# Decoder layer on one core: attention probabilities scaled by their row's reciprocal sum on GpSimd before the transposes, instead of the attention output scaled by transposed reciprocals

## What is computed

```
qp = q @ Wq.T                         # q: layernorm(x), 16 heads of 32
kv = latent_kv @ Wkv_expand.T         # the context; k, v = split(kv)
scores = einsum('bhqd,bhkd->bhqk', qh, kh) / sqrt(32), causal mask (512 x 512)
attn = softmax(scores, axis=-1)
out = einsum('bhqk,bhkd->bhqd', attn, vh)
return out @ Wout.T
```

## Time and profile before

| | |
|---|---|
| time, 3 runs | median 1807.98 us (1806.97 to 1808.12) |
| the profiled execution's own time | 1807.13 us |
| its span, first to last instruction | 1805.3 us |
| PE busy | 1412.3 us (78% of the span) |
| DVE busy | 1217.4 us (67%) |
| ACT busy | 842.5 us (47%) |
| POOL busy | 546.0 us (30%) |
| chain that ended last, by engine | PE 47%, DVE 25%, issue 9%, POOL 6%, ACT 5% |
| costliest lines of that chain | L513 9%, L1094 7%, L1111 7%, L1148 6%, L1171 6%, L1132 5%; L1120 has 2% |
| cross-attention stage of one batch, 605 to 701 us | PE busy 87.6 us, ACT 55.1, DVE 51.2, POOL 0.0 |

### The profile page before, as it was taken

The page is one execution under the profiler, slowest core; times in us unless marked ns, Lnnn a source line. Parts: engine busy times, 40 slices in busy tenths (PEclk is TensorE's granted clock), DMA queues, the critical chain, the costliest instruction groups (busy, mean ns, idle before and its releaser), DMA issues.

```text
span 1805.3 us, 31768 instructions
## 1 busy us (share of the span) xinstructions
PE 1412.3 (78%) x11547; PEld 875.8 (49%) x11616; DVE 1217.4 (67%) x2539; ACT 842.5 (47%) x2066; POOL 546.0 (30%) x494
## 2 busy tenths in 40 slices
PE   1224899779987899779887998779877988789866
PEld 0113665346644665446544664446544664456523
DVE  8993455975579555975578555965588556965565
ACT  2541354455634464445634554445544554445422
POOL 5881000650046101640046101640056002630054
PEclk9999799898989799898989799888989799889987
DMA  5311000010000000010000000010000000000000
GB/s 181 115 42 36 1 1 24 7 25 1 2 24 13 18 1 25 7 25 1 1 24 13 19 1 24 7 24 1 2 24 18 13 1 24 7 19 1 1 6 18
DMA packets 25287, 36.10 MB, mean 20 GB/s; under 512 B 2480, under 2 KB 10672, under 8 KB 25136
## 3 DMA queue, kind: packets, MB, share of 16 engines
q1 hardware_dynamic: 25136, 34.09, 7.0%
HBM read 25.69 MB, written 8.39 MB: 19 GB/s over the span
## 4 chain that ended last, share of the span: by engine, by line
PE 47%; DVE 25%; issue 9%; POOL 6%; ACT 5%; DMA 0%; SPq 0%; DVEq 0%; ACTq 0%; POOLq 0%
PE psum L513 9%; PE psum L1094 7%; PE psum L1111 7%; PE psum L1148 6%; PE psum L1171 6%; PE psum L1132 5%; DVE top L805 4%; DVE nmx L755 3%; DVE inter L831 3%; DVE xn L507 3%; PE psum L1097 2%; POOL iq L677 2%; DVE pt L768 2%; PE psum L1120 2%; DVE q L801 2%
## 5 line engine op out<-in xcount | busy, mean ns | idle before, releaser
L502 POOL TENSOR_TENSOR rstd<-var_eps,minus_half 128x1 f32<-128x1 f32 x96 | 55.2, 575 | 889.7 <-DVE var_eps L496 889.7
L953 ACT ACTIVATE p<-psum,nmx 128x384 f32<-128x384 f32 (+3 forms) x512 | 265.8, 526 | 68.8 <-DVE nmx L755 64.4
L755 DVE TENSOR_REDUCE nmx<-psum 128x2 f32<-128x256 f32 (+3 forms) x256 | 210.7, 823 | 115.7 <-PE psum L1097 115.6
L768 DVE COPY pt<-psum 128x128 f32<-128x128 f32 (+3 forms) x256 | 124.6, 487 | 194.0 <-PE psum L1111 193.5
L1111 PE MATMUL psum<-ident,p 128*128 128x128 f32 x1280 | 206.9, 289 | 19.6 <-ACT pt L977 16.4
L1094 PE MATMUL psum<-k_hl,q_hl 32*128 32x128 f32 (+3 forms) x1536 | 207.0, 377 | 15.4 <-DVE q_hl L742 11.7
L677 POOL TENSOR_TENSOR inter<-inter,rscale 128x512 f32<-128x512 f32 x128 | 140.0, 1094 | 205.0 <-DVE rscale L839 201.3
L977 ACT COPY pt<-psum 128x128 f32<-128x128 f32 (+3 forms) x256 | 109.2, 427 | 141.8 <-PE psum L1111 140.4
L1111 PEld LDWEIGHTS psum<-ident,p 128*128 128x128 f32 x1280 | 144.2, 146 | 54.6 <-ACT pt L977 25.8
L1171 PE MATMUL psum<-wg_sb,xq_t 128*128 128x512 bf16 x452 | 135.3, 421 | 37.8 <-ACT xq_t L984 24.7
L1094 PEld LDWEIGHTS psum<-k_hl,q_hl 32*128 32x128 f32 x1536 | 126.8, 203 | 76.6 <-issue 53.8
(11 more groups left out here) (102 smaller groups left out, 2497.5 us busy)
## 6 DMA issues: line engine op xcount, KB each, us to landing
x_in<-in_x_dram SPq DMA_DIRECT2D x32, 256.0 KB, 4.0
out_dram<-x_res SPq DMA_DIRECT2D x64, 128.0 KB, 2.4
w_raw<-in_w_gate_dram SPq DMA_DIRECT2D x16, 256.0 KB, 2.7
w_raw<-in_w_up_dram SPq DMA_DIRECT2D x16, 256.0 KB, 3.0
w_raw<-in_w_down_dram SPq DMA_DIRECT2D x16, 256.0 KB, 3.8
ctx_in<-in_ctx_t_dram SPq DMA_DIRECT2D x8, 256.0 KB, 3.0
wq_raw<-in_wq_t_dram SPq DMA_DIRECT2D x1, 1024.0 KB, 8.1
wo_sb<-in_wo_t_dram SPq DMA_DIRECT2D x1, 1024.0 KB, 10.1
```

Source lines behind the costliest of these rows:

```text
L755: dve.tensor_reduce(nmx2[:, u % UNITS, 2 * pr:2 * pr + 2], where(("scores2", oc, qt, pr))[:, :, 0:(qt + 1) * P], AX_X, ALU.max, negate=Tru ...
L768: free(dve.tensor_copy(pt2[:, hh, 0:m], where(label)[:, 0, 0:m]), label)
L953: ins = act.activation(p2[:, (4 * u + hh) % P2_RING, 0:m], where(label)[:, hh % 2, 0:m], ACT.Exp, bias=nmx2[:, u % UNITS, hh:hh + 1], accu ...
```

## The change

The probabilities are divided by their row sums before they are transposed, on GpSimd, in place in `p2`. DVE's `recips` takes a pair of heads at a time and signals GpSimd; GpSimd's new `scale_probs` multiplies each head's 128 x m tile by its column of reciprocals, and PE's transpose of a head waits for that head's product. The transposed reciprocals and all that served them are gone (`recip_x`, `recip_t`, `turn_recip`, `take_recip`, their places in slot C1); `take_out` becomes a copy. The ring `p2` has 8 places. On DVE the reciprocals of pair 1 of unit u now stand between `maxima(u+1, 0)` and `take_probs(u, 0)`, those of pair 0 of unit u+1 ahead of `maxima(u+1, 1)`.

```diff
@@ -38,7 +38,7 @@
...
 INTER_LAG = 3
-P2_RING = 6
+P2_RING = 8
 RAW = 3
...
@@ -84,7 +84,6 @@
...
                     plan[f"C{hh % 2}"].append(("probsT2", oc, qt, hh))
-                plan["C1"].append(("recipT", oc, qt))
         for t in range(T):
...
@@ -700,9 +697,20 @@
...
+                def scale_probs(u, pr):
+                    oc, qt = units[u]
+                    m = (qt + 1) * P
+                    pool.wait_ge(S["rcp2_ready"], 2 * u + pr + 1)
+                    for hh in (2 * pr, 2 * pr + 1):
+                        p = p2[:, (4 * u + hh) % P2_RING, 0:m]
+                        pool.tensor_scalar(p, p, rcp2[:, u % UNITS, hh:hh + 1], None, ALU.mult).then_inc(S["p2_ready"], 1)
+
                 for i in range(P1_STEPS):
...
                 for b in range(B):
+                    for u in range(b * UNITS, (b + 1) * UNITS):
+                        for pr in range(2):
+                            scale_probs(u, pr)
                     last = b + 1 == B
...
@@ -767,21 +775,15 @@
...
-                def recips(u):
+                def recips(u, pr):
                     oc, qt = units[u]
-                    until_freed(dve, ("scores2", oc, qt, 0))
-                    until_freed(dve, ("scores2", oc, qt, 1))
-                    link(dve.reciprocal(rcp2[:, u % UNITS, :], sum2[:, u % UNITS, :]))
-                    if u >= 2:
-                        until_filled(dve, ("recipT", *units[u - 2]))
-                    dve.tensor_copy(recip_x[:, u % 2, :].rearrange("p (h d) -> p h d", h=4),
-                                    rcp2[:, u % UNITS, :].unsqueeze(2).to_broadcast([P, 4, HD])).then_inc(S["rx_ready"], 1)
+                    until_freed(dve, ("scores2", oc, qt, pr))
+                    heads = slice(2 * pr, 2 * pr + 2)
+                    dve.reciprocal(rcp2[:, u % UNITS, heads], sum2[:, u % UNITS, heads]).then_inc(S["rcp2_ready"], 1)
...
                     until_filled(dve, ("outT", oc))
-                    until_freed(dve, ("recipT", oc, T - 1))
-                    free(dve.tensor_tensor(out_n[:, oc % OC, :], where(("outT", oc))[:, 0, :],
-                                           recip_t[:], ALU.mult), ("outT", oc))
+                    free(dve.tensor_copy(out_n[:, oc % OC, :], where(("outT", oc))[:, 0, :]), ("outT", oc))
...
@@ -867,11 +869,13 @@
...
                         maxima(first, pr)
+                    recips(first, 0)
                     for u in range(first, end):
...
                             maxima(u + 1, 0)
+                        recips(u, 1)
                         take_probs(u, 0)
...
@@ -880,9 +884,9 @@
...
                         if u + 1 < end:
+                            recips(u + 1, 0)
                             maxima(u + 1, 1)
                         take_probs(u, 1)
-                        recips(u)
                     take_out((b + 1) * OC - 1)
...
@@ -955,16 +959,6 @@
...
                             free(ins, label)
-                        else:
-                            ins.then_inc(S["p2_ready"], 1)
-
-                def take_recip(u):
-                    oc, qt = units[u]
-                    label = ("recipT", oc, qt)
-                    until_filled(act, label)
-                    if oc and qt == 0:
-                        until_freed(act, ("outT", oc - 1))
-                    free(act.copy(recip_t[:, qt * P:(qt + 1) * P], where(label)[:, 0, 0:P]), label)
...
@@ -1017,8 +1011,6 @@
...
                         oc, qt = units[u]
-                        if u > first:
-                            take_recip(u - 1)
                         more = oc % OC + 1 < OC
...
@@ -1030,8 +1022,6 @@
...
                             exps(u + 1, 1)
-                    take_recip(end - 1)
-
                     last = b + 1 == B
...
@@ -1103,21 +1093,12 @@
...
                         until_free(pe, label)
-                        if hh % 2:
-                            until_freed(pe, ("scores2", oc, qt, hh // 2))
-                        else:
-                            pe.wait_ge(S["p2_ready"], 2 * u + hh // 2 + 1)
+                        pe.wait_ge(S["p2_ready"], 4 * u + hh + 1)
                         for kt in range(qt + 1):
...
                         fill_done(last, label)
-
-                def turn_recip(u):
-                    label = ("recipT", *units[u])
-                    until_free(pe, label)
-                    pe.wait_ge(S["rx_ready"], u + 1)
-                    fill_done(pe.transpose(where(label)[:, 0, 0:P], recip_x[:, u % 2, :], ident[:]), label)
...
@@ -1219,7 +1200,6 @@
...
                         if u > first:
-                            turn_recip(u - 1)
                             values2(u - 1)
...
@@ -1232,7 +1212,6 @@
...
                             output(b * T, [0, 1] if qt == 1 else [2])
-                    turn_recip(end - 1)
                     values2(end - 1)
...
```

More of the change, by code:

```diff
@@ L165, in decoder_layer @@
         rcp2 = sb("rcp2", [P, OC * T, 4])
-        recip_t = sb("recip_t", [P, N])
-        recip_x = sb("recip_x", [P, 2, P])
         def phase(*wanted):
@@ L237, in decoder_layer @@
             "q_high", "k_high",
-            "nmx_ready", "p2_ready", "values_done", "rx_ready",
+            "nmx_ready", "rcp2_ready", "p2_ready", "values_done",
             "scale_x", "x_scaled", "q8x_ready", "xq_ready",
```

## The result

The changed kernel takes 1863.6 us (median of 4 runs, 1857.2 to 1872.8) against 1807.5 us before; the ratio is 1.0325 with a 95% interval of 1.0303 to 1.0347. It is 56 us slower, where 30 us less were forecast; the range ended at 1801. The profiled execution took 1857.2 us (span 1855.3), that is 50 us more than the one of before.

The account below looks back on a forecast made before the run. PE was taken to set the stage's pace. Gains of 4.11 us a batch, less 3 x 0.13 and 0.01 of waits, made 3.71, 29.7 in all, so 1778 us; range 1758 to 1801.

Parts of the forecast that it names:

- The product's duration: GpSimd's product of one 128x512 head, T, between exp and transpose: taken as 0.86 us, range 0.53 to 1.32.
- all four bounds: Limits for T from other GpSimd instructions in the trace: 0.53 and 0.86 us, 1.09 and 1.32 us.
- The slower rival: T above 1.32 us makes the kernel slower, 64 us for each us of T, 1839 at T = 1.8; chance 0.10.
- The waits for the product: PE's waits for GpSimd at three qt = 3 units a batch, each 2T - 1.59, 0.13 us at T = 0.86.
- tail: The stage's last unit: 0.50 us a batch gained if nothing waits, with the product 0.50 - 2(T - 0.605), -0.01 at 0.86.
- Its own sign of being wrong: Among the signs of error: PE waits for GpSimd at smaller units, a queue behind reciprocals that DVE gives late.
- The clock: Rival: one stretch more or less per batch at half clock, 18 us, giving 1796 or 1760; chances 0.05 and 0.07.
- The removal's terms: Gains from dropping the transposed reciprocals, before new waits: 0.69 + 0.78 + 1.74 + 0.90 = 4.11 us a batch.
- The term of nothing at qt = 1: Groups 2 and 3 and group 4's two middle units: PE's 0.84 us wait for ACT's copy grows, so no gain counted.
- In the first group 0.90 us: Group 1 at half clock, units qt = 1 and 2: each saves the transpose's 0.45 us, 0.90 us a batch.
- The shared way to SBUF: Rival: GpSimd blocks DVE's copies of the four largest units by 0.85 us each, 27 us lost, 1805; chance 0.03.
- Faster, 0.84: Chance given to the change being faster by more than about 0.2% (3.6 us).

Follow-up runs that it names:

- e4: The changed kernel with GpSimd's product written as tensor_tensor with the reciprocal broadcast along the row; 1777.6 us, ratio 0.9841.
- e1: The changed kernel without GpSimd's products, PE's transposes waiting for DVE's reciprocals instead, output left undivided; 1748.0 us, ratio 0.9683.
- e7: The changed kernel with DVE taking the reciprocals of the next unit's pair 0 earlier at qt = 2, ahead of its copy; 1886.2 us, ratio 1.0452.
- e5: The changed kernel with the products moved from GpSimd to DVE, right behind the reciprocals; 1806.8 us, ratio 1.0014.
- e3: The changed kernel with the product over only a quarter of each head's columns, the others left undivided; 1743.1 us, ratio 0.9662.
- e9: The changed kernel with transposes of a constant on PE in its waits for GpSimd, at qt = 3 and the last unit; 1827.9 us, ratio 1.0133.
- e10: The tensor_tensor kernel (e4) with constant transposes in PE's waits at qt = 1 of groups 2 and 3 and in the last unit; 1757.2 us, ratio 0.9735.
- e11: The kernel before the change with constant transposes where PE waits for ACT's copy and for the spread reciprocals; 1779.4 us, ratio 0.9865.
- e12: e10 with ten more constant transposes where PE waits for a batch's first queries; 1754.9 us, ratio 0.9718.

## Why the prediction was wrong

**The product's duration**, taken as 0.86 us, was the step that turned the sign. It measured 1.563 us, beyond all four bounds. The mistake was to believe that the rows of other instructions bound one that isn't there. That this step alone turns the sign is shown by e4, where the same product in 1.04 us leaves a gain of 27 us, and by the sum itself, which at T = 1.563 gives a loss of 15 us. The slower rival had the rule right, that T beyond 1.32 is a loss; it had a chance of 0.10, and its 64 us for each us of T measured 165 (e4 to the changed kernel).

**The waits for the product** were about right in their sum, and wrong in their places. With T = 1.563 the prediction's own formulas give 3 x (3.126 - 1.59) = 4.61 us of waits at the group ends, a tail of 0.50 - 2 x 0.958 = -1.42, and 4.11 - 4.61 - 1.42 = -1.92 us a batch, so 15 us slower. Of a product that lasts no time to one of 1.563 us that is 4.61 + 1.92 = 6.5 us a batch; PE's idle time in the stage rose by 6.3 from e1 (6.1) to the changed kernel (12.4). But a group end has 1.16 us of waits and not 1.54, and 2.9 us a batch of waits for GpSimd lie at smaller units, which the prediction had put at nothing but for 0.3 in the first unit. Its own sign of being wrong, waits at smaller units, came true, in the fourth group above all. The tail lost 3.4 us in the mean of the batches (last unit, from its second scores, 9.05 and 12.47 us), against 1.42. e7 shows that the chain at a group end is the one that was written down: exps, reciprocals, two products.

**The clock** was the second wrong step, and it hit both sides of the sum. It had been made a rival of 18 us either way, with chances of 0.05 and 0.07, without a tie to the product's length. It comes behind PE's waits: with longer waits the changed kernel's low time went up from 357 to 423 us, and keeping PE busy took it back to 339 and gave 36 us. Those 66 us of low time are at most 33 us of time. How the 56 us split between waits and clock is not shown to the us. In the profiled executions 36 of the 50 us are PE's added idle time in the stages, 3 its added busy time there, although the transposes are gone, and 11 lie outside the stages, where the clock of the output projection fell. Part of the 20 us by which the gain was priced too low (37 forecast for a product that costs nothing, 57 in e1) is the clock as well: low time 357 to 304 us, at most 26 us.

**The removal's terms** held roughly in groups 2 and 3, 1.5 us each beside the clock where 1.20 were summed. The term of nothing at qt = 1 held in these two groups: PE waits there 0.75 us for ACT's copy in e4 and 0.96 in e1, against 0.84. In the fourth group it rested on a wrong reading. Its two middle units have no such wait of 0.84 us in the kernel before: at qt = 1 PE doesn't wait for ACT at all, at qt = 2 only the 0.23 us shown above. In e1 the term still comes out near nothing, since PE waits 0.47 and 0.34 us for ACT there. In the changed kernel these two units hold 1.74 us of waits for GpSimd. In the first group 0.90 us were summed and 0.3 came: 0.45 us was the distance of weight loads, while on PE the transpose took 0.35 (613.25 to 613.60), and PE waited 0.1 us longer for the exps in e1. That this group would go at half speed to its query projection held (15.9 us before, 15.6 after).

**The shared way to SBUF** was rightly given little. DVE's copies beside GpSimd:

```profile
L776 DVE COPY pt<-psum x256: 271/480/692, 200.6 to 1749.7; 128x128 f32<-128x128 f32 x32, 128x256 f32<-128x256 f32 x32, 128x384 f32<-128x384 f32 x32, 128x512 f32<-128x512 f32 x32
```

Before, their median was 486 ns and their longest 693 ns. The Trainium skill (SBUF — State Buffer, "Who interferes with whom") leaves a DVE instruction with at most one SBUF input and outside the two-port modes free of GpSimd; the row agrees. The Trainium skill (GPSIMD Engine Reference, section 3.1) gives 769 ns for 512 elements in a tight loop at its best; this product takes 1563, and the measurement decides. The remark of the Trainium skill (the same page, section 8) that VectorE is about twice as fast for elementwise work was on the right side: 1563 against 483 ns (e5) is a factor of 3.2.

**Faster, 0.84**, was far too sure. The cost that decided was one that no row showed, so the forecast's sign stood on an analogy. That e4 (1778 us) lands on the forecast 1778 is luck: its product is slower than the 0.86 us of the forecast, which costs more than was summed, and the removal gave more.

Left open: why e3, with short products, was 5 us faster than e1 without any; what the larger ring and the dropped copies on DVE and ACT gave, which no run takes apart; and when a wait lets the clock fall and when it doesn't. e7 shows that the same waits (66.3 and 67.9 us) can come with 492 or 423 us of low time.

## What to carry to other kernels

When work is put on an engine that hasn't run that instruction form in the kernel, its duration is the prediction: time the form first, and try the equivalent ones, here a broadcast tensor_tensor for a per-row tensor_scalar, 1.04 us for 1.56. Ask of every operation that is put between two engines at which units its time is covered, at the small ones too. Price a short wait of PE at more than its own length: transposes of a constant gave back 36 us where they stood in waits of 45 us in all (e9), 20 us for 20 (e10) and 26 us for 45 (e11). If such a wait can't be removed, a few matmuls of a constant into a slot that is overwritten anyway are worth a try.

## What the runs showed of the hardware

- GpSimd multiplies a 128x512 float32 tile by a per-row scalar in 1563 ns (603 for 128x128), by the same column broadcast as a second operand in 1041 ns (402). DVE takes 483 ns (284).
- PE's clock fell from 1.00 to half within a few us of waits of 0.4 and 0.9 us (e7), and stayed there in group 1 for some 13 us, from 600 us on with PE busy throughout (e12). The rise lies in the group's long projection there, and in e7 a few us behind the fall. The Trainium skill (TensorE: Matmul & The Clock Gate, Part 1) describes the half rate as the state of rest, which activity lifts. That idle moments lower the clock agrees with e7 and e9; that a busy engine is lifted soon does not hold for group 1.
- Transposes of a constant in the waits kept the clock up: low time 423 to 339 us (e9), 336 to 280 (e10), 357 to 291 (e11).
